# Latent attention in a Flamingo-style block: one normalisation for two, and the value product cut in half

## What is computed

```python
x = x + tanh(g_xattn[1]) * _L1_xattn_ref(ctx, _layernorm(x), gamma_x, beta_x, gamma_l, beta_l, Wq, Wkv, Wo)

def _L1_xattn_ref(x, latents, ...):        # 8 heads of 64
    xn = layer_norm(x, gamma_x, beta_x)        # of the context
    ln = layer_norm(latents, gamma_l, beta_l)  # a second norm: the latents are normalised already
    q = ln @ Wq
    k_x, v_x = split(xn @ Wkv); k_x = rope_rotate_k(k_x)
    k_l, v_l = split(ln @ Wkv)
    k, v = concat([k_x, k_l]), concat([v_x, v_l])   # 256 keys per sequence
    return softmax(q @ k.T * scale) @ v @ Wo
```

## Time and profile before

| | us |
|---|---|
| median of 3 runs (lowest, highest) | 920.49 (919.72, 921.42) |
| the profiled execution's own time | 919.85 |
| its span, first to last instruction | 918.1 |
| PE busy in the span | 765.5 (83%) |
| DVE, ACT, POOL busy | 601.6, 497.4, 428.4 |
| the stage of the change on PE, about | 240 to 486 |

### The profile page before, as it was taken

The page is one execution under the profiler, slowest core; times in us unless marked ns, Lnnn a source line. Parts: engine busy times, 40 slices in busy tenths (PEclk is TensorE's granted clock), DMA queues, the critical chain, the costliest instruction groups (busy, mean ns, idle before and its releaser), DMA issues. The chain is left out here.

```text
span 918.1 us, 21278 instructions
## 1 busy us (share of the span) xinstructions
PE 765.5 (83%) x6415; PEld 582.6 (63%) x6415; DVE 601.6 (66%) x1816; ACT 497.4 (54%) x1344; POOL 428.4 (47%) x767
## 2 busy tenths in 40 slices
PE   3999996999679998888987876999969667659991
PEld 1565565798456776767764754666649445439991
DVE  5899995244467887777855556999957727623433
ACT  1576664676246765566662651777764322226663
POOL 3246665100534556565534327666316706724541
PEclk9999997899799999999999997899999875569996
DMA  7999940342100000000001541100000330112215
GB/s 258 382 403 404 296 166 28 78 95 68 24 7 14 13 14 25 13 26 14 14 19 54 126 121 30 25 19 24 4 1 2 96 112 32 47 51 62 72 52 153
DMA packets 69279, 78.97 MB, mean 86 GB/s; under 512 B 12848, under 2 KB 58560, under 8 KB 68912
## 3 DMA queue, kind: packets, MB, share of 16 engines
q1 hardware_dynamic: 55760, 60.64, 20.5%
q0 software_dynamic: 6368, 13.38, 5.0%
q10 hardware_dynamic: 7040, 3.58, 1.4%
HBM read 31.61 MB, written 45.96 MB: 84 GB/s over the span
## 5 line engine op out<-in xcount | busy, mean ns | idle before, releaser
L1398 PE MATMUL banks<-exps,work 128*128 128x128 f32 x718 | 106.2, 284 | 15.5 <-ACT exps L1458 10.4
L330 POOL DMA_INDIRECT routed_region<-routed_lines,line_slots x96 | 96.0, 1000 | 29.4 <-issue 25.3
L1398 PEld LDWEIGHTS banks<-exps,work 128*128 128x128 f32 x718 | 91.3, 194 | 22.2 <-ACT exps L1458 16.1
L774 ACT ACTIVATE probs_keymajor<-banks 128x512 f32<-128x512 f32 x128 | 69.9, 595 | 37.3 <-PE banks L584 37.3
L265 POOL TENSOR_TENSOR small<-small,half_and_eps 128x1 f32<-128x1 f32 x144 | 82.6, 573 | 11.3
L550 PE MATMUL banks<-work 32*128 32x512 f32 x256 | 78.8, 693 | 4.2 <-DVE exps L667 3.2
L658 DVE TENSOR_REDUCE small<-banks 128x8 f32<-128x1024 f32 x64 | 77.5, 1211 | 4.9 <-PE banks L557 3.7
L667 DVE TENSOR_TENSOR exps<-banks,small 128x1024 f32<-128x1024 f32 x64 | 77.7, 1215 | 0.4
L362 POOL DMA_INDIRECT late_results<-routed_region,line_slots x64 | 63.3, 990 | 24.8 <-issue 23.8
L584 PE MATMUL banks<-consts,exps 128*128 128x128 f32 x512 | 72.8, 288 | 1.1 <-ACT work L805 1.1
L584 PEld LDWEIGHTS banks<-consts,exps 128*128 128x128 f32 x512 | 59.4, 149 | 18.6 <-issue 12.3
(11 more groups left out here) (274 smaller groups left out, 1834.4 us busy)
## 6 DMA issues: line engine op xcount, KB each, us to landing
routed_region<-mid SPq DMA_DIRECT2D x52, 528.0 KB, 5.5
exps<-routed_region SPq DMA_DIRECT2D x125, 66.0 KB, 2.0
weights_f<-in_weights_f SPq DMA_DIRECT2D x1, 4096.0 KB, 17.7
routed_region<-work SPq DMA_DIRECT2D x63, 64.0 KB, 1.8
weights_f<-in_weights_f SPq DMA_DIRECT2D x3, 1024.0 KB, 10.7
shifted_rows<-work SPq DMA_DIRECT2D x16, 128.0 KB, 1.8
work<-expert_results SPq DMA_DIRECT2D x8, 256.0 KB, 4.6
routed_region<-routed_lines,line_slots POOLq DMA_INDIRECT x96
```

Source lines behind the costliest of these rows:

```text
L330: nc.gpsimd.indirect_dma_start(k.regions[layer % 2], bass.IndirectOffsetOnAxis(k.slots[:, b, j:j + 1], 0), k.line[:, b % LINES, j, :], Non ...
L774: nc.scalar.activation(k.pT[:, g * 512:(g + 1) * 512], bank[:, PT + g % 2, :], ACT.Copy).then_inc(s.pT, 1)
L1398: last = nc.tensor.matmul(bank[:, 2 + m % 4, i * T:(i + 1) * T], tile.weights[:, m % COPIES, i * 128:(i + 1) * 128], tile.gotT[:, m % 2, : ...
```

## The change

Three things, all in latent_attention. First, x is normalised once, straight to lh: with v the variance of x, two norms in a row equal one with v(1 + eps) + eps^2 under the root, so POOL's first step becomes a tensor_scalar (multiply, add) in place of a tensor_tensor. The tile xh, its statistics, dev_latent on POOL and norm_latent on DVE go. norm_in makes lh where it made xh; POOL's dev_in does lh's and the context's deviation. Second, pv is cut: pv(0) (heads 0 to 3) stays behind query, pv(2) (heads 4 to 7) comes behind logits, ahead of values(1), and it alone signals s.pv. Third, the values lie in three slots instead of two, and the emptying of values(0) and values(1) waits for pv of b - 3 instead of b - 2.

```diff
@@ -248,7 +248,10 @@
     return t
-def layer_norm_steps(nc, k, sem, st, mv, rstd):
+def layer_norm_steps(nc, k, sem, st, mv, rstd, twice=False):
@@ -260,7 +263,11 @@
     def deviation(pool, s, n):
         wait(pool, sem.stats, n)
-        nc.gpsimd.tensor_tensor(rstd[:, s, 0:1], mv[:, s, 1:2], k.half[:, 1:2], ALU.add).then_inc(sem.var_eps, 1)
+        if twice:
+            nc.gpsimd.tensor_scalar(rstd[:, s, 0:1], mv[:, s, 1:2], 1.0 + EPS, EPS * EPS, ALU.mult,
+                                    ALU.add).then_inc(sem.var_eps, 1)
+        else:
+            nc.gpsimd.tensor_tensor(rstd[:, s, 0:1], mv[:, s, 1:2], k.half[:, 1:2], ALU.add).then_inc(sem.var_eps, 1)
         wait(pool, sem.var_eps, n)
         nc.gpsimd.tensor_tensor(rstd[:, s, 1:2], rstd[:, s, 0:1], k.half[:, 0:1], ALU.pow).then_inc(sem.rstd, 1)
@@ -865,33 +872,32 @@
     s = Semaphores()
     (s.ch, s.lh, s.v, s.inT, s.q, s.k_ctx, s.k_lat, s.exp, s.scores, s.k1, s.kvT, s.t1, s.k3, s.t2,
      s.q1, s.v1, s.norm, s.pT, s.oT, s.ptr, s.pv, s.added, s.logits_out, s.out, s.xh2, s.xs2, s.xT2,
-     s.logits, s.inv, s.max, s.nmax, s.xh, s.kept, s.halved) = sems.new("a1", """
+     s.logits, s.inv, s.max, s.nmax, s.kept, s.halved) = sems.new("a1", """
         ch lh v inT q k_ctx k_lat exp scores k1 kvT t1 k3 t2 q1 v1 norm pT oT ptr pv added logits_out
-        out xh2 xs2 xT2 logits inv max nmax xh kept halved""")
+        out xh2 xs2 xT2 logits inv max nmax kept halved""")
     c, cols, bank, w = k.c, k.cols, k.bank, k.work
     MA, MB, PT = 6, 7, 4
     qT = w[:, 0:1024].rearrange("p (s h t) -> p s h t", s=2, h=L1P)
     kT = w[:, 2048:4096].rearrange("p (s h t) -> p s h t", s=2, h=L1P)
-    v = w[:, 4096:6144].rearrange("p (s i n) -> p s i n", s=2, i=2)
+    v = [w[:, from_:from_ + 1024].rearrange("p (i n) -> p i n", i=2) for from_ in (4096, 5120, 1024)]
     kvT = w[:, 6144:6656].rearrange("p (s t) -> p s t", s=2)
     t1, t2 = w[:, 6656:7168], w[:, 7168:7680]
     oT = w[:, 7680:8192]
     by_half = {"wk1": k.w["wkrot1"], "wq1": k.w["wk1"]}
     m = k.mid
-    ch, xh, lh, xh2, xs2 = (split(m[:, n * 256:(n + 1) * 256], 128) for n in range(5))
+    ch, lh, xs2 = (split(m[:, n * 256:(n + 1) * 256], 128) for n in (0, 2, 4))
     mx = split(k.small[:, 0:16], L1H)
     nmx = split(k.small[:, 16:32], L1H)
     sums = split(k.small[:, 32:48], L1H)
     inv = split(k.small[:, 48:64], L1H)
-    sc, sx, sl2, so = (norm_names(sems, "a1_" + n) for n in ("ctx", "x", "lat", "out"))
+    sc, sl2, so = (norm_names(sems, "a1_" + n) for n in ("ctx", "lat", "out"))
     routing_names(sems, "a1", s)
     choose, place, rank, begin, count, mark, send = routing_steps(nc, k, s, ld, E1, 1)
     then = following(s)
     s.half, s.late = sems.new("a1", "half late")
     fetch, add_late = late_steps(nc, k, s, ld, 0)
     stats_c, dev_c, norm_c = layer_norm_steps(nc, k, sc, *norm_scratch(k.small, 64))
-    stats_x, dev_x, norm_x = layer_norm_steps(nc, k, sx, *norm_scratch(k.small, 96))
-    stats_l, dev_l, norm_l = layer_norm_steps(nc, k, sl2, *norm_scratch(k.small, 128))
+    stats_l, dev_l, norm_l = layer_norm_steps(nc, k, sl2, *norm_scratch(k.small, 128), twice=True)
     stats_o, dev_o, norm_o = layer_norm_steps(nc, k, so, *norm_scratch(k.small, 160))
     tg = k.tg[:, 1:2]
     SCALE = L1D ** -0.5
@@ -964,18 +970,24 @@
                         last.then_inc(s.ptr, 1)
                 return stage
-            def pv(b, sl):
+            def pv(p0):
+                def stage(b, sl):
+                    pv_pairs(b, sl, p0)
+                return stage
+            def pv_pairs(b, sl, p0):
                 wait(pe, s.pT, b * 4 + 4)
                 wait(pe, s.v, 2 * b + 2)
-                for p in range(L1P):
+                for p in range(p0, p0 + 2):
                     for i in range(2):
                         for par in range(2):
                             h = 2 * p + par
                             n = 2 * (h % 4) + h // 4
                             last = nc.tensor.matmul(bank[64 * par:64 * par + 64, PT, p * T:(p + 1) * T],
-                                                    v[:, sl, i, h * L1D:(h + 1) * L1D],
+                                                    v[b % 3][:, i, h * L1D:(h + 1) * L1D],
                                                     k.pT[:, (2 * n + i) * T:(2 * n + i + 1) * T], start=i == 0, stop=i == 1)
-                last.then_inc(s.pv, 1)
+                if p0:
+                    last.then_inc(s.pv, 1)
             def out(b, sl):
                 wait(pe, s.oT, b + 1)
@@ -1020,8 +1032,8 @@
             pe.wait_ge(s.halved, 4)
             done(pe)
             walk(pe, [(scores(0), 1), (in_T, 0), (scores(1), 1), (k_ctx, 0), (out, 3), (shared_gate(0), 3),
-                      (probs(0), 2), (k_lat, 0), (probs(2), 2), (next_T, 4), (query, 0), (pv, 2), (values(0), 0),
-                      (logits, 4), (values(1), 0), (ranks, 5), (shared_up, 3), (shared_gate(1), 4)])
+                      (probs(0), 2), (k_lat, 0), (probs(2), 2), (next_T, 4), (query, 0), (pv(0), 2), (values(0), 0),
+                      (logits, 4), (pv(2), 2), (values(1), 0), (ranks, 5), (shared_up, 3), (shared_gate(1), 4)])
             then.tensor(pe)
         @block.vector
@@ -1056,31 +1068,24 @@
             def values(b, sl):
                 wait(dve, s.v1, 2 * b + 1)
-                wait(dve, s.pv, b - 1)
-                nc.vector.tensor_copy(v[:, sl, 0, :], bank[:, MA, :]).then_inc(s.v, 1)
+                wait(dve, s.pv, b - 2)
+                nc.vector.tensor_copy(v[b % 3][:, 0, :], bank[:, MA, :]).then_inc(s.v, 1)
             def add(b, sl):
                 wait(dve, s.out, b + 1)
-                wait(dve, s.xh, b + 1)
+                wait(dve, s.lh, b + 1)
                 nc.vector.scalar_tensor_tensor(at(k.x, b), bank[:, MB, 0:D], tg, at(k.x, b), ALU.mult,
                                                ALU.add).then_inc(s.added, 1)
             def stats_in(b, sl):
                 add_late(dve, b)
-                stats_x(dve, at(k.x, b), sl, b + 1, s.xh)
+                stats_l(dve, at(k.x, b), sl, b + 1, s.lh)
                 stats_c(dve, at(k.ctx, b), sl, b + 1, s.ch)
             def norm_in(b, sl):
-                wait(dve, s.lh, b - 1)
-                norm_x(dve, xh[:, sl, :], at(k.x, b), sl, b + 1).then_inc(s.xh, 1)
                 wait(dve, s.inT, b - 1)
+                norm_l(dve, lh[:, sl, :], at(k.x, b), sl, b + 1).then_inc(s.lh, 1)
                 norm_c(dve, ch[:, sl, :], at(k.ctx, b), sl, b + 1).then_inc(s.ch, 1)
-                wait(dve, s.xh, b + 1)
-                stats_l(dve, xh[:, sl, :], sl, b + 1, s.lh)
-            def norm_latent(b, sl):
-                wait(dve, s.inT, b - 1)
-                norm_l(dve, lh[:, sl, :], xh[:, sl, :], sl, b + 1).then_inc(s.lh, 1)
             def stats_out(b, sl):
                 wait(dve, s.added, b + 1)
@@ -1103,18 +1108,15 @@
             add_bias(dve)
             walk(dve, [(normalise, 4), (rope_sin, 2), (rope_cos, 2), (norm_out, 6), (add, 5), (maximum, 3),
-                       (stats_out, 5), (norm_in, 1), (chosen, 7), (norm_latent, 1), (values, 2), (logits, 6),
+                       (stats_out, 5), (norm_in, 1), (chosen, 7), (values, 2), (logits, 6),
                        (stats_in, 0), (placed, 7)])
             then.vector(dve)
         @block.gpsimd
         def _(pool):
             def dev_in(b, sl):
-                dev_x(pool, sl, b + 1)
+                dev_l(pool, sl, b + 1)
                 dev_c(pool, sl, b + 1)
-            def dev_latent(b, sl):
-                dev_l(pool, sl, b + 1)
             def dev_out(b, sl):
                 dev_o(pool, sl, b + 1)
@@ -1143,7 +1145,7 @@
             begin(pool)
             pool.wait_ge(ld.empty[1], 32 * REGIONS[1])
-            walk(pool, [(dev_out, 7), (dev_in, 2), (rope_add, 3), (keep, 9), (dev_latent, 2), (counted, 9),
+            walk(pool, [(dev_out, 7), (dev_in, 2), (rope_add, 3), (keep, 9), (counted, 9),
                         (fetched, 0), (sent, 9)])
             then.gpsimd(pool)
@@ -1200,8 +1202,8 @@
             def values(b, sl):
                 wait(act, s.v1, 2 * b + 2)
-                wait(act, s.pv, b - 1)
-                nc.scalar.activation(v[:, sl, 1, :], bank[:, MA, :], ACT.Copy).then_inc(s.v, 1)
+                wait(act, s.pv, b - 2)
+                nc.scalar.activation(v[b % 3][:, 1, :], bank[:, MA, :], ACT.Copy).then_inc(s.v, 1)
             act.wait_ge(ld.weights[2], 16)
             for n, name in enumerate(("wk1", "wq1")):
```

## The result

The changed kernel takes 910.56 us (median of 4 runs, 909.43 to 911.85), the kernel before 920.11 beside it (4 runs, 915.76 to 921.42): a ratio of 0.9885, 95% interval 0.9851 to 0.9919. It is faster by 1.2%, where 898 us, 2.4%, were forecast. The profiled execution took 911.85, with a span of 910.1; so 8.0 us (918.1 - 910.1) are to be found between the two profiles, and 22.3 were forecast.

The account below looks back on a forecast made before the run. PE's serial work was taken to bound the attention stage, so only its idle time could be won. Gains of 1.75 + 13.2 + 7.4 = 22.3 us gave 898 us; own range 893 to 903, widened to 892 to 912.

Parts of the forecast that it names:

- What bounds the kernel: Attention stage: PE is close to full, so time is won only where PE stands idle.
- The start: Start of the stage: without DVE's third norm the first in_T starts earlier, 1.75 us gained, bounds 0 and 2.48.
- POOL's new place: POOL's transfers follow keep at once, 3.3 us earlier, so transposes and DVE's long L1035 are clear of the second scatter.
- So the long steps become short ones: 13.2 us: Seven steps with gathers and scatters shrink to the short step's 13.09 us; 13.2 us gained, bounds 0 and 14.
- the hold: Seven long steps: a PE result falling into POOL's second scatter is seen by its reader some 0.8 us after it.
- the halving: pv in two halves closes PE's 0.66 us gap ahead of values(1): 0.55 a step, 7.4 us in all, bounds 3 and 10.4.
- rival (a): Hold belongs to the burst of four transfers and moves with it to values(0), values(1) or exps: 911 us, chance 0.12.
- rival (d): Slower: any PE result during the burst is held, now over query, values(0) and values(1), 1.5 us each: 930 us, chance 0.06.
- the rest of the kernel: After the stage everything moves ahead as a whole: no gain, 3 us either way for clock changes.
- The widened range: Whole kernel: 892 to 912 us, stretched to reach rivals at 905.5 and 911 and come to 8 in 10.
- The clock: After idle time TensorE falls from 2.4 to 1.2 GHz for a while: 1.7 us of PE's busy time in a step.

Follow-up runs that it names:

- the gathers apart: POOL's gathers moved to behind dev_in, away from the scatters: in the kernel before (two normalisations) 913.76 us, in the changed kernel 904.99 us.
- with the gathers last: Changed kernel with the two scatters ahead of the two gathers, still four transfers in a row: 902.23 us, ratio 0.9809.
- gathers alone: Steps without scatters in the changed kernel with each gather issued twice, four gathers in a row: 939.76 us, ratio 1.02.
- with the pause: Changed kernel with POOL's dev_out (0.86 us) issued between the two gathers and the two scatters: 901.85 us, ratio 0.9786.

## Why the prediction was wrong, step by step

**What bounds the kernel: right.** The stage is as long as PE's work and PE's idle time; with the idle time gone, seven steps last as long as PE is busy (88.97 and 88.14).

**The start: 1.75 forecast, 1.92 seen, but only half of it is the edit's.** PE's idle time ahead of in_T falls from 2.48 to 1.57, 0.91. The other 1.0 is the product ahead of it, which starts at 233.03 instead of 234.04, and that drifts: from 231.97 to 236.74 among the profiles of the experiments. In five of them with one normalisation the idle time is 1.09 and ends with ACT's work on weights (L852). Against the 2.48 the edit is worth 0.9 to 1.4. (In one profile with two normalisations, the gathers apart, the wait is 4.05.)

**POOL's new place: right.** The first gather follows keep (336.97 + 0.28 = 337.25) and counted (337.22 + 0.23) by 0.17, and the transposes and the long L1047 are clear of the burst, as forecast.

**"So the long steps become short ones: 13.2 us": this step failed.** It rested on reading the hold as belonging to the second scatter and to what falls into it. The burst did leave in_T, but on its new place lay values(0), and 2.17 came instead of 13.2 and the halving's 3.85. The runs show in its place: under four transfers in a row a result of PE is taken up late at each place that the row was given, in_T by 1.02 to 1.75 in the kernel before, values(0) by 1.28 to 2.72 in the changed one, with the scatters last, with the gathers last (1.14 to 1.88), and in two of five steps with gathers alone (2.28 and 2.32). With the gathers apart, or with 0.86 us of POOL's work between the pairs, values(0) is taken up after 0.04. The first attention's hold, the evidence against rival (a), was true and misread: a pair holds as well, but for 0.7 (the keys, twice above), not 2.7.

The prediction's own times would have shown the new collision. It puts the second scatter at 406.35, so the first lies from about 405.0 to 406.0. values(0) ends at 406.28 in that step of the kernel before and 0.95 earlier behind half a pv: near 405.3, inside that scatter. The hand-overs that it checked at the new place were POOL's own and the transposes; that of values(0) it checked nowhere but in the rivals.

The row that rival (d) held against itself, a gather over the end of values(0) that does no harm, was read as if nothing followed. That gather is the first of a burst of four; the two scatters come behind it:

```profile
332.80 1.02 POOL L330 DMA_INDIRECT routed_region<-routed_lines,line_slots  x1 [0.30 <-issue]
334.13 1.00 POOL L330 DMA_INDIRECT routed_region<-routed_lines,line_slots  x1 [0.30 <-issue]
```

All seven bursts of the kernel before begin shortly before values(0) ends, 0.56 or 0.57 in five of them, 0.98 and 1.34 in the other two, and values(0) is taken up after 0.03 to 0.05 each time. In the changed kernel they begin 2.9 to 3.1 before. So not every result under a burst is late: beside the first transfer values(0) was on time, in the third it was not. The edit took it from the harmless end of the burst into its middle.

**Rival (a) gave the mechanism, and its time by some luck.** It said that a hold that belongs to the burst of four moves with it, on to values(0), values(1) or exps, at 911; the result is 910.56. With 0.12 it was underrated. What could have raised it stands in the prediction itself: the hold in this stage occurred only in steps with all four, seven times in seven. But its 911 is made of 1.75 and 7.4. By the table above the start and all steps gave 5.7 of that 9.15 (1.92 - 0.12 + 1.71 + 2.17), and 2.3 came from the rest of the kernel, which it put at 0. The widened range, 892 to 912, holds the result because of this rival; the forecast's own, 893 to 903, does not.

**The halving: the mechanism right, its size 0.45 instead of 0.55.** The gap of 0.66 is gone. From pv(0) to values(1) PE takes 314.99 - 311.76 = 3.23, where 3.07 were forecast from 3.81: each half of pv costs 1.02 up to the next product, not 0.95. From values(1) to scores(0) it is 316.25 - 314.99 = 1.26 against 1.14. So 3.81 - 3.23 - 0.12 = 0.46 a step. The value product alone gives the same in its short steps. The forecast's 3.6 for the seven steps without all four came to 1.71 for two more reasons: the second step, counted with 0.46, is 12.49 in both kernels, and the one behind the last of the seven is 13.39 long at a granted clock of 0.94.

**The clock.** After the idle time in a long step TensorE falls from 2.4 to 1.2 GHz for a while: the step from 346.55 has a granted clock of 0.93 and 13.56 of PE's busy time, one at 1.00 has 12.63. In the seven steps PE is busy for 90.59 in the changed kernel and 88.14 with the pause, at 1.00; so 2.4 us of the hold's price come by the clock, from the three steps with clocks of 0.93 to 0.95. The two profiles of the changed kernel, 102.65 and 97.96 for the same seven steps, differ by 0.7 of PE's busy time and by 4.0 of its idle time, that is by how long values(0) is held.

**The rest of the kernel: 2.3 us faster, forecast 0,** inside the 3 us left for the clock.

**Rival (d), slower, was not idle either.** The normalisation alone is slower than the kernel before: seven holds as before, at a place where one costs 2.52 instead of 1.51. And the two edits don't add: +5.0, -2.3 (by its interval no difference) and -9.6 us for the first, the second and both, medians against the kernel before, run beside each. That each edit moves the burst against the chain accounts for it: the held result and its delay differ in all three (the table above).

## What to carry to other kernels

When a wait is explained by two things that lie over each other, an edit that moves one of them doesn't end it until the trace shows what they will lie over next; write down every hand-over at the new place and price the same wait there. Before such an edit is judged, order the issuing engine's own small work between the transfers, so that the hand-over on the longest path falls into the gap: here 0.86 us of it, moved within the order, was worth as much as the whole change (911.4 to 901.9, after 921.1 to 911.4). And two edits on one path are not measured by adding them up, when both shift a third thing.

## What was not expected of the hardware

A result of PE that is finished while POOL issues indirect transfers in a row can be taken up late by its reader: by 0.68 and 0.74 us in the rows shown under a pair, by up to 2.7 under four. In the changed kernel the reader starts between 0.6 before and 0.9 after the last transfer's end. The Trainium skill (SBUF — State Buffer, "Who interferes with whom") has PE and ACT waiting on nobody. Here ACT starts late on a result of PE while POOL issues transfers (347.85 above), and since it does so just as DVE does, the port pair that DVE shares with GpSimd would not explain these rows. Whether any port is at work no row shows.

Open is what carries the hold, since the traces show only when a reader starts: whether PE's product or the signal of it is late. Open too is which results are hit. Three steps with four gathers were spared, wholly or nearly (0.04, 0.13 and 0.78). In two steps of the kernel before, values(1) ends 0.31 and 0.64 into the third transfer of four, and ACT takes it up after 0.04. It isn't a matter of transfers running at the same time alone: with the pause values(1) ends at 340.43 (339.31 + 1.12), half a us into the second scatter, and ACT takes it up at 340.63, 0.2 later. Six of the seven steps are like this; in the one that is 13.08 long it is 0.94, so the pause makes the hold harmless and does not abolish it.

```profile
339.31 1.12 PE L955 MATMUL banks<-weights_a,work 128*128 128x512 f32 x2
339.93 0.99 POOL L337 DMA_INDIRECT routed_region<-routed_lines,line_slots  x1 [0.30 <-issue]
...
340.63 0.60 ACT L1206 ACTIVATE work<-banks 128x512 f32<-128x512 f32 x1 [0.19 <-PE banks L955]
```
